# Graph attention on one core: rows 0 and 1 multiplied together strip by strip, statistics by pairs of tiles, the values' sum in four column groups, inlayer2 loaded sooner

## The chip, the core and the metric

The kernel runs on one core of one Trainium2 chip. The time is device microseconds of the whole kernel; three runs of the kernel before gave a median of 1459.9 us (1458.99 to 1459.92).

## The reference, cut to what matters

```python
N, D, H = (8192, 256, 128)
# values: h = relu(layernorm(x))            (8192 x 256)
h = jnp.maximum(_layernorm(x, axis=-1), 0.0)
# two numbers per node, from another input and small weights
g  = inlayer2 @ W.T + b
f1 = g @ w1 + b1
f2 = g @ w2 + b2
logits = f1[:, None] + f2[None, :]
bias_mat = NEG_BIG * (1.0 - (adj > 0).astype(jnp.float32))
coefs = softmax(leaky_relu(logits, 0.01) + bias_mat, axis=-1)   # 8192 x 8192
out = x + coefs @ h
```

The adjacency is 8192 x 8192 of int32 (268 MB). A node without a neighbour takes the mean of all values.

## The kernel before, in words

The exponential of a leaky ReLU of a sum splits into products of a row factor and a column factor, so the weight of a pair is `min(max(b_word, c_word), mask)` (times a factor that is put into the values). Output rows are worked on in 64 tiles of 128 ("row I"). A row has two chunks (c = 0, 1) of 4096 columns, a chunk four parts (g = 0 to 3) of 1024 columns of words and four strips. A strip (k = 0 to 7) is eight tiles of 128 neighbours.

For each row the steps are these.

- SP loads the adjacency of a chunk in four transfers of 512 KB (`load_adj`, L286) once ACT has read the chunk of the row before (`m_ready`).
- ACT turns a part of the adjacency into a mask (`mask_part`, L451). At the end of a row it scales the accumulator (`scale_rows`, L458).
- DVE makes the weights of a part (`weights`, L706) and transposes a strip of them into one of four buffers (`turn`, L716), which waits for PE to be done with the strip four earlier (`mm_done`).
- PE multiplies a strip (`products`, L892 and L894): 24 matmuls of 257 columns, three for each tile, since a weight is a bf16 high half and an f16 low half and a value is two f16 parts.
- POOL adds x and the mean's share (`finish`, L399 to L404), and SP stores the tile.

Four buffers between DVE and PE are all that decouples them. The accumulator `acc` has two halves, one for even and one for odd rows.

Ahead of the loop, and mixed with row 0, the kernel makes everything that the rows need:

- `inlayer2` comes in eight strips (L281, queues of SP and ACT, 8 transfers of 256 KB for two strips). DVE transposes each (`turn_in2`, L601), PE multiplies it (`f_of_strip`, L856: 8 matmuls, for strip k of them in two passes), ACT copies the result in two chunks (`f_to_sbuf`, L434). `chunk_f` (L632 to L637) brings f into columns and finds its maximum, which goes over PE (L877, L879) to the shifted `f2_rel` (L671). From there ACT makes the exponentials (L513, L439, L520), and DVE packs them into words (`pack`, L695 and L696).
- x comes in eight strips too. For strips 0 and 1 ACT makes sums and squares (L485). For the others DVE runs one `bn_stats` for each tile of 256 columns (`raw_stats`, L644), and `mean_var` aggregates eight tiles (L651, L653). POOL makes the inverse roots and the affine factors (`rstds`, `affine`).
- The values are made by half strips, n = 0 to 15: ACT applies the affine step and the ReLU (`values(n)`, L472, four instructions), then the f16 high part is cast (`high_of_values`: odd n on ACT, L478, even n on DVE, L683), and the low part is the difference (`low_of_values`: odd n on DVE, L690, even n on POOL, L392). POOL writes one more column of each tile (`D_column`, L385).
- In row 0 PE waits for both parts of strip k, and behind each strip's products it adds the strip's values over all nodes (`sum_of_values`, L903: 16 matmuls with 2 columns of weights and 256 columns of values). From them comes the mean (`h_sum`, L827, then L920).

The order of all this is written out by hand in each engine's program, as a list of calls (`high_of_values(0)`, `weights(0, 0, 0)`, `raw_stats(44, 48)`, ...). Engines run their lists in that order, so a wait holds up everything behind it on its engine. PE does all of row 0 and then row 1:

```python
for k in range(NS):
    if k == NS - 1:
        pe.wait_ge(scaled, I)
    if is_row(I, 0):
        for part in (hi_ready, hi_act_ready, lo_ready, lo_dve_ready, D_column_ready):
            pe.wait_ge(part, k + 1)
    products(I, par, k)
    if is_row(I, 0):
        mm = sum_of_values(k)
```

Of the kernel before, what the change touches and what calls it, by code (L numbers as in the profile page):

```python
# [35 lines left out]
P = 128  # L36
# [9 lines left out]
def graph_attention(nc, x, adj, inlayer2, W, b, w1, b1, w2, b2, out):  # L46
# [26 lines left out]
    with ExitStack() as ctx:  # L73
# [33 lines left out]
        stats = sb("stats", [P, ROWS, 6], F32)  # L107
        mv = sb("mv", [P, ROWS, 2], F32)
# [18 lines left out]
        h_sum = sb("h_sum", [2, D], F32)  # L127
# [13 lines left out]
        hs_ps = small[0:2, 1, 0:D]  # L141
# [56 lines left out]
        zeroed = sem("zeroed")  # L198
        ident_ready = sem("ident_ready")
# [24 lines left out]
        packed = sem("packed")  # L224
# [3 lines left out]
        neg_mul_ready = sem("neg_mul_ready")  # L228
        D_parts_ready = sem("D_parts_ready")
# [45 lines left out]

        block = ctx.enter_context(nc.Block())
# [33 lines left out]
        def _(sp):  # L310
# [3 lines left out]
            first_loads(sp, (0, 1))  # L314
            first_adj(sp, 0, (0, 1))
# [5 lines left out]
            def body(I, par, half):  # L321
                for n in range(NS):
                    if n % Q == Q - 1 and not is_row(I, ROWS - 1):
                        sp.wait_ge(m_ready, 8 * I + (n + 1))
# [14 lines left out]
        def _(pool):  # L339
# [6 lines left out]
            rstd_order = (0, 2, 3, 1, 4, 5, 6, 7)  # L346

            def rstds(k):
                at = slice(TS * k, TS * (k + 1))
                if k < AS:  # L350
                    pool.wait_ge(x_passes, TS * (AS + k + 1))
# [14 lines left out]
            def affine(k):  # L366
# [8 lines left out]
                else:  # L375
# [3 lines left out]
                    nc.gpsimd.tensor_tensor(h_add[:, at], mv[:, at, 0], neg_mul[:, at],  # L379
                                            ALU.mult).then_inc(h_affine_ready, 1)  # L380

# [6 lines left out]
            def low_of_values(n):  # L388

                pool.wait_ge(h_ready, HALF * (n + 1))  # L390
                pool.wait_ge(hi_ready, n // 2 + 1)
# [15 lines left out]
            for k in (0, 2, 3, 1):  # L407
                rstds(k)
            scale_D()
            for k in range(4):  # L410
                affine(k)
            low_of_values(0)
            rstds(4)
            affine(4)
            D_column(0)
            for k in range(1, NS):
                low_of_values(2 * k)
                if k + 4 < NS:
                    rstds(k + 4)
                    affine(k + 4)  # L420
                D_column(k)
# [4 lines left out]
        def _(act):  # L426
# [9 lines left out]
            def b_of_chunk(c):  # L436

                act.wait_ge(b_ps_ready, c + 1)
# [3 lines left out]
            def mask_part(I, g, c):  # L442
                if not is_row(I, 0):
                    act.wait_ge(p_ready, 8 * I + (Q * c + g - 7))
# [115 lines left out]
            for g in range(Q):  # L560
                mask_part(1, g, 1)
# [382 lines left out]
```

## Time and profile before

| | us |
|---|---|
| median of 3 runs | 1459.9 |
| the profiled execution's own time | 1460.0 |
| its span in the trace | 1458.2 |
| PE busy | 1414.1 (97%) |
| DVE busy | 1286.4 (88%) |
| ACT busy | 613.0 (42%) |
| POOL busy | 252.8 (17%) |

Between the span and the execution's own time lie 1.8 us that belong to no instruction. A row of the trace gives the start in us from the span's beginning, the length, the engine and line, the operation, what it writes and reads, how many are merged (x), and in brackets how long the engine was idle ahead of it and who ended that. Instructions of an engine overlap a little, so one of many costs the distance between two starts and not its length. PEclk is the clock that was granted to TensorE: 1.00 is 2.4 GHz and 0.50 is 1.2 GHz.

### The profile page before, as it was taken

The page shows a single profiled execution, that of the slowest core. Times are in us where ns is not written, and L with a number is a line of the kernel's source. Part 1 is how long each engine was busy: PE and PEld are TensorE (multiplying, and loading weights), DVE is VectorE, ACT ScalarE, POOL GpSimd, SP SyncE. Part 2 cuts the span into 40 slices and gives each one's busy share as a digit, 9 for nine tenths or more (in the row PEclk, how much of TensorE's full clock was granted, in tenths as well). Part 3 has the DMA queues.
Part 4 walks back from the last instruction along what each step waited for, and adds up shares of the span by engine and source line. Part 5 has one row for each costly group of instructions (what it writes and reads, how often), then busy time and mean ns, then how long its engine had stood idle before and what let it go on. Part 6 is the DMA issues. An engine that isn't in the chain of part 4 may idle for free.

```text
span 1458.2 us, 33394 instructions
## 1 busy us (share of the span) xinstructions
PE 1414.1 (97%) x12585; PEld 1248.4 (86%) x12585; DVE 1286.4 (88%) x1396; ACT 613.0 (42%) x722; POOL 252.8 (17%) x249
## 2 busy tenths in 40 slices
PE   7479999999999999999999999999999999999998
PEld 6358888888888888888888888888888888888887
DVE  5899998989898989989898989899898989898894
ACT  1794444444343444434343444444343434444430
POOL 0371111111011111111110111111011101111111
PEclk9789999999999999999999999999999999999999
DMA  9959999999999999999999999999999999999940
GB/s 293 295 117 197 229 231 232 234 231 212 210 215 207 213 209 214 210 209 215 209 211 208 215 209 212 211 214 209 210 214 209 210 207 218 209 210 212 211 106 8
DMA packets 110164, 302.36 MB, mean 207 GB/s; under 512 B 11716, under 2 KB 44612, under 8 KB 110148
## 3 DMA queue, kind: packets, MB, share of 16 engines
q1 hardware_dynamic: 100720, 291.68, 89.5%
q10 hardware_dynamic: 9428, 10.49, 2.4%
q8 instruction: 8, 0.13, 0.0%
q14 instruction: 8, 0.07, 0.0%
HBM read 293.73 MB, written 8.39 MB: 207 GB/s over the span
## 4 chain that ended last, share of the span: by engine, by line
PE 92%; ACT 2%; SPq 2%; DMA 2%; DVE 1%; issue 1%; POOL 0%; POOLq 0%; ACTq 0%; DVEq 0%
PE acc L892 61%; PE acc L894 30%; SPq L281 2%; ACT h_f L472 1%; DMA H<-in_x_dram 1%; DMA adj_sb<-in_adj_dram 1%; ACT o_room L472 1%; DVE wgt L706 0%; ACT H L478 0%; PE rp L864 0%; DVE stats L644 0%; DVE wgt L632 0%; ACT rp L451 0%; DVE H L690 0%; DVE mv L651 0%
## 5 line engine op out<-in xcount | busy, mean ns | idle before, releaser
L892 PE MATMUL acc<-H,wT 128*128 128x257 f16 x8192 | 1354.6, 273 | 19.1 <-DVE wT L716 19.1
L894 PE MATMUL acc<-H,wT 128*128 128x257 f16 x4096 | 1119.4, 273 | 0.0
L892 PEld LDWEIGHTS acc<-H,wT 128*128 128x128 bf16 x8192 | 801.6, 98 | 121.4 <-issue 21.3
L451 ACT ACTIVATE mask<-adj_sb 128x1024 bf16<-128x1024 int32 x504 | 520.0, 1054 | 552.9 <-DVE wgt L706 441.3
L716 DVE STREAM_TRANSPOSE wT<-wgt 128x1024 f32<-128x1024 f32 x512 | 633.7, 1238 | 132.9 <-PE acc L894 132.7
L706 DVE SCALAR_TENSOR_TENSOR wgt<-b_word,c_word,mask 128x1024 f32<-128x1024 f32 x504 | 627.9, 1257 | 0.0
L894 PEld LDWEIGHTS acc<-H,wT 128*128 128x128 f16 x4096 | 401.2, 98 | 50.2
L399 POOL TENSOR_TENSOR x_res<-o_room,x_res 128x256 f32<-128x256 f32 x64 | 66.4, 1037 | 1131.3 <-ACT o_room L458 1100.8
L458 ACT ACTIVATE o_room<-acc,r_den 128x256 f32<-128x256 f32 x64 | 30.3, 473 | 246.2 <-DVE r_den L735 246.2
L404 POOL TENSOR_TENSOR o_room<-o_room,x_res 128x256 f32<-128x256 f32 x64 | 81.0, 1265 | 5.3
L401 POOL TENSOR_SCALAR o_room<-h_mean,no_nb 128x256 f32<-128x256 f32 x64 | 62.1, 970 | 0.0
L856 PE MATMUL rp<-wT,h_f 128*128 128x256 f32 x128 | 30.8, 407 | 3.6 <-DVE h_f L609 3.6
L856 PEld LDWEIGHTS rp<-wT,h_f 128*128 128x128 f32 x128 | 26.3, 207 | 7.9 <-DVE h_f L609 3.7
L472 ACT ACTIVATE h_f<-H,h_add,h_mul 128x256 f32<-128x256 f32 x48 | 24.7, 587 | 0.0
L392 POOL TENSOR_TENSOR H<-h_f,H 128x1024 f16<-128x1024 f32 x8 | 20.5, 2567 | 11.1 <-DVE H L683 9.4
L644 DVE BATCH_NORM_STATS2 stats<-H 128x6 f32<-128x256 f32 x48 | 16.9, 418 | 3.7 <-DMA H<-in_x_dram 3.7
L601 DVE STREAM_TRANSPOSE wT<-wgt 128x1024 f32<-128x1024 f32 x8 | 9.5, 1222 | 8.5 <-PE rp L856 4.4
L725 DVE TENSOR_SCALAR no_nb<-acc 128x1 f32<-128x1 f32 x64 | 7.6, 118 | 9.2 <-PE acc L894 9.2
L903 PE MATMUL small<-H,D_inv_parts 128*2 128x256 f16 x128 | 15.4, 273 | 0.0
L485 ACT ACT_TABLE_LOAD x1 | 1.3, 1283 | 31.3 <-issue 31.3
L357 POOL TENSOR_TENSOR rstd<-var_eps,minus_half 128x8 f32<-128x8 f32 x8 | 13.2, 1646 | 7.0 <-DVE var_eps L653 6.8
L903 PEld LDWEIGHTS small<-H,D_inv_parts 128*2 128x2 f16 x128 | 10.1, 84 | 4.8 <-issue 1.9
(88 smaller groups left out, 159.2 us busy)
## 6 DMA issues: line engine op xcount, KB each, us to landing
adj_sb<-in_adj_dram SPq DMA_DIRECT2D x508, 512.0 KB, 8.5
x_res<-in_x_dram SPq DMA_DIRECT2D x64, 128.0 KB, 4.0
out_dram<-o_room SPq DMA_DIRECT2D x64, 128.0 KB, 4.3
H<-in_x_dram ACTq DMA_DIRECT2D x16, 256.0 KB, 12.7
H<-in_x_dram SPq DMA_DIRECT2D x16, 256.0 KB, 13.6
wgt<-in_L_gnn_inlayer_dram ACTq DMA_DIRECT2D x8, 256.0 KB, 9.8
wgt<-in_L_gnn_inlayer_dram SPq DMA_DIRECT2D x8, 256.0 KB, 10.6
adj_sb<-in_L_gnn_inlayer_dram ACTq DMA_DIRECT2D x8, 256.0 KB, 12.5
```

The lines of the kernel that those rows point to most:

```text
L281: eng.dma_start(stage[B * q:B * (q + 1), :, :], source[k // SC, k % SC, q]).then_inc(signal, 16)
L399: nc.gpsimd.tensor_tensor(x_res[:, par, :], o_raw[:, par, :], x_res[:, par, :], ALU.add).then_inc(pool_step, 1)
L401: nc.gpsimd.tensor_scalar(o_sb[:, par, :], h_mean[:, :], no_nb[:, par:par + 1], None, ALU.mult).then_inc(pool_step, 1)
L404: nc.gpsimd.tensor_tensor(o_sb[:, par, :], o_sb[:, par, :], x_res[:, par, :], ALU.add).then_inc(o_ready, 1)
L451: nc.scalar.activation(place, adj_sb[:, c, g * CQ:(g + 1) * CQ], ACT.Relu, scale=M_SCALE).then_inc(m_ready, 1)
L458: nc.scalar.activation(o_raw[:, par, :], acc[:, par, 0:D], ACT.Copy, scale=r_den[:, par:par + 1]).then_inc(scaled, 1)
L472: nc.scalar.activation(h_slot(n)[:, t, :], x_stage(n // 2)[:, j % TS, :], ACT.Relu, scale=h_mul[:, j:j + 1], bias=h_add[:, j:j + 1]).then_ ...
L706: nc.vector.scalar_tensor_tensor(out=wgt[:, c, g, :], in0=b_word[:, c * CQ:(c + 1) * CQ], scalar=c_word[:, bass.ds(Q * I + g, 1)], in1=sho ...
L716: nc.vector.transpose(wT[:, k % 4, :, :].rearrange("p t (g r) -> p g t r", g=Q), wgt[:, c, :, s * SQ:(s + 1) * SQ]).then_inc(t_ready, 1)
L856: mm = pe.matmul(rp[:, k // SC, SQ * (k % SC):SQ * (k % SC + 1)], V[:, m, :], in2T[:, k % 2, m, :], start=(m == 0), stop=(m == FM - 1))
L892: pe.matmul(acc[:, par, 0:DV], w_hi[:, k % 4, t, :], H[:, j, part, 0:DV], start=(j == 0 and part == 0), stop=False)
L894: mm = pe.matmul(acc[:, par, 0:DV], w_lo[:, k % 4, t, :], H[:, j, 0, 0:DV], start=False, stop=(j == ROWS - 1))
```

## The change

- **Order of rows 0 and 1.** Two tables set the order in which parts of weights and strips of products of rows 0 and 1 are made. PE no longer finishes row 0 first. Weights of row I go to `wgt[:, I]` for these two rows, and masks, weights, turns and values stand in new lists on ACT, DVE and POOL. All four masks of a chunk are requested by the new numbering (`nth_part`).
- **Statistics.** One `bn_stats` reads two tiles at a time, column by column alternately from one and the other, so that its statistics of even and odd elements are those of the two tiles. The aggregates (`bn_aggr`) are gone: `variance` makes `var_eps` by one instruction per strip. Numbers: 24 `bn_stats` of 512 elements for 48 of 256, and no `bn_aggr` for 48.
- **Sum of the values.** The 16 matmuls of a strip write to four column groups (PSUM partitions 0, 32, 64, 96 and the one behind each), consecutive ones to different groups. DVE zeroes the 128 partitions first, `h_sum` has 128 partitions, and the mean's matmul sums over all of them.
- **Loads.** The eight strips of inlayer2 are requested before x's strips 1 to 3. ACT requests 18 of its 256 KB transfers before its first computation, where it requested 24, and the others one or two at a time between later work. Its half of the second chunk of row 0's adjacency comes after ten steps of masks and values.
- **Who does what.** Of the 16 high parts ACT makes 12 and DVE 4 (before 8 and 8). The two parts of D and D_inv go from DVE to POOL. Chunk 1 of b is made before chunk 0.
- **Rows 0 to 2 at the seam.** The finish of row 0 stands on DVE right behind the last turn of row 1, `scale_rows(0)` on ACT behind the masks (2, g, 0), and the masks (2, g, 1) behind that.

```diff
+        two_rows = ((0, 0, 0), (0, 1, 0), (0, 2, 0), (0, 3, 0), (0, 0, 1), (0, 1, 1), (1, 0, 0), (1, 1, 0),
+                    (1, 2, 0), (1, 3, 0), (0, 2, 1), (0, 3, 1), (1, 0, 1), (1, 1, 1), (1, 2, 1), (1, 3, 1))
+        strip_order = ((0, 0), (0, 1), (0, 2), (0, 3), (1, 0), (1, 1), (1, 2), (0, 4),
+                       (1, 3), (0, 5), (1, 4), (1, 5), (0, 6), (0, 7), (1, 6), (1, 7))
...
         def first_loads(eng, quadrants):
             load_in2(eng, 0, 4, quadrants)
             load_x(eng, 0, 1, quadrants)
-            load_in2(eng, 4, 6, quadrants)
-            load_x(eng, 1, 2, quadrants)
-            load_in2(eng, 6, 8, quadrants)
-            load_x(eng, 2, 4, quadrants)
+            load_in2(eng, 4, 8, quadrants)
...
-                for j in range(first, end):
+                for j in range(first, end, 2):
                     if j == first or j % TS == 0:
                         dve.wait_ge(xs_loaded[j // TS], 64)
-                    nc.vector.bn_stats(out=stats[:, j, :], in_=x_stage(j // TS)[:, j % TS, :]).then_inc(stats_ready, 1)
-
-            def mean_var(k):
+                    nc.vector.bn_stats(out=pair_stats[:, j // 2, :],
+                                       in_=x_stage(j // TS)[:, j % TS:j % TS + 2, :].rearrange("p t d -> p d t")
+                                       ).then_inc(stats_ready, 1)
+
+            def variance(k):
...
             def products(I, par, k):
-                pe.wait_ge(t_ready, 8 * I + (k + 1))
+                pe.wait_ge(t_ready, nth_strip(I, k))
+                if is_row(I, 0):
+                    pe.wait_ge(hi_ready, k // 2 + 1)
+                    pe.wait_ge(hi_act_ready, 2 * (k + 1) - (k // 2 + 1))
+                    for part in (lo_ready, lo_dve_ready, D_column_ready):
+                        pe.wait_ge(part, k + 1)
...
-                for j in range(TS * k, TS * (k + 1)):
-                    for part in range(2):
-                        mm = pe.matmul(hs_ps, D_inv_parts[:, j, :], H[:, j, part, 0:D],
-                                       start=(j == 0 and part == 0), stop=(j == ROWS - 1 and part == 1))
+                if k == 0:
+                    pe.wait_ge(D_parts_ready, 2)
+                    pe.wait_ge(hs_zeroed, 1)
+                for part in range(2):
+                    for j in range(TS * k, TS * (k + 1)):
+                        a = B * (j % Q)
+                        mm = pe.matmul(hs_ps[a:a + 2, :], D_inv_parts[:, j, :], H[:, j, part, 0:D],
+                                       start=(j < Q and part == 0), stop=(j >= ROWS - Q and part == 1))
                 return mm
 
+            for I, k in strip_order:
+                products(I, I, k)
+                if I == 0:
+                    mm = sum_of_values(k)
+                    if k == NS - 1:
+                        mm.then_inc(h_sum_done, 1)
```

How the order moves on DVE between the last turn of inlayer2 and `f2_rel`, before:

```order
L601 STREAM_TRANSPOSE wT<-adj_sb 128x4x8x32 x8
L644 BN_STATS stats<-H 128x6 x12
L651 BN_AGGR mv<-stats 128x2 x8
L653 TENSOR_SCALAR var_eps<-mv 128x8
L632 STREAM_TRANSPOSE wgt<-mask 128x1024
L633 COPY f_col<-wgt 128x64
L635 TENSOR_REDUCE tiny<-f_col 128x1
L644 BN_STATS stats<-H 128x6 x3
L632 STREAM_TRANSPOSE wgt<-mask 128x1024
```

and in the changed kernel:

```order
L679 STREAM_TRANSPOSE wT<-adj_sb 128x4x8x32 x8
L712 STREAM_TRANSPOSE wgt<-mask 128x1024
L713 COPY f_col<-wgt 128x64
L715 TENSOR_REDUCE tiny<-f_col 128x1
L726 BN_STATS stats<-H 128x6 x4
L712 STREAM_TRANSPOSE wgt<-mask 128x1024
```

Fifteen statistics and eight aggregates stood ahead of the second transposition of `chunk_f`, and now four paired statistics do.

DVE around the first turns of the products' weights (L716), before:

```order
L690 TENSOR_TENSOR H<-h_f,H 128x4x256
L706 SCALAR_TENSOR_TENSOR wgt<-b_word,c_word,rp 128x1024
L644 BN_STATS stats<-H 128x6 x4
L716 STREAM_TRANSPOSE wT<-wgt 128x4x8x32
L706 SCALAR_TENSOR_TENSOR wgt<-b_word,c_word,rp 128x1024
L683 CAST H<-h_f 128x4x256
L690 TENSOR_TENSOR H<-o_room,H 128x4x256
```

and in the changed kernel, from its third weights (L789) to its third turn (L799):

```order
L789 SCALAR_TENSOR_TENSOR wgt<-b_word,c_word,acc 128x1024
L789 SCALAR_TENSOR_TENSOR wgt<-b_word,c_word,rp 128x1024
L769 TENSOR_TENSOR H<-h_f,H 128x4x256
L799 STREAM_TRANSPOSE wT<-wgt 128x4x8x32
L726 BN_STATS stats<-H 128x6 x2
L799 STREAM_TRANSPOSE wT<-wgt 128x4x8x32
L734 TENSOR_SCALAR var_eps<-stats 128x8
L799 STREAM_TRANSPOSE wT<-wgt 128x4x8x32
```

In both the first turn comes behind four weights and one low part. Before, weights of chunk 1, values and statistics came ahead of the second turn, and now the second and third turn follow with one paired statistics and a variance between them.

ACT's queue from the loads of inlayer2 (L281) to its first computation, before:

```order
L281 DMA wgt<-in_L_gnn_inlayer_dram 32x8x256 x8
L281 DMA H<-in_x_dram 32x8x256 x2
L281 DMA adj_sb<-in_L_gnn_inlayer_dram 32x8x256 x4
L281 DMA H<-in_x_dram 32x8x256 x2
L281 DMA adj_sb<-in_L_gnn_inlayer_dram 32x8x256 x4
L281 DMA H<-in_x_dram 32x8x256 x4
L485 ACT_TABLE_LOAD
```

and in the changed kernel:

```order
L310 DMA wgt<-in_L_gnn_inlayer_dram 32x8x256 x8
L310 DMA H<-in_x_dram 32x8x256 x2
L310 DMA adj_sb<-in_L_gnn_inlayer_dram 32x8x256 x8
L547 ACT_TABLE_LOAD
L547 ACTIVATE o_room,x_sum<-H 128x256 x8
```

The six requests for x's strips 1 to 3 no longer stand ahead of the table load.

## Rows read from the trace of the kernel before

**Rows 1.** The page: busy time, the chain, and the weight loads of the sums
```profile
PE 1414.1 (97%) x12585; PEld 1248.4 (86%) x12585; DVE 1286.4 (88%) x1396; ACT 613.0 (42%) x722; POOL 252.8 (17%) x249
...
PE 92%; ACT 2%; SPq 2%; DMA 2%; DVE 1%; issue 1%; POOL 0%; POOLq 0%; ACTq 0%; DVEq 0%
...
L903 PEld LDWEIGHTS small<-H,D_inv_parts 128*2 128x2 f16 x128 | 10.1, 84 | 4.8 <-issue 1.9
```
**Rows 2.** Windows: time; busy PE, PEld, DVE, ACT, POOL; PEclk; DMA share; GB/s
```profile
70.00:80.00 10.00, 0.36 (x2) 0.29 (x3) 9.86 (x25) 9.53 (x17) 7.26 (x9) 0.50 0.78 175
...
121.59:142.70 21.11, 21.11 (x193) 18.79 (x193) 21.11 (x23) 8.16 (x9) 2.83 (x3) 1.00 1.03 225
...
1410.80:1431.90 21.10, 21.10 (x194) 18.77 (x192) 18.89 (x20) 1.22 (x2) 3.34 (x3) 1.00 0.04 12
```
**Rows 3.** Timeline of PE, 0 to 150 us
```profile
14.29 30.84 PE L856 MATMUL rp<-wT,h_f 128*128 128x256 f32 x128 [3.62 <-DVE h_f L609]
...
79.64 0.59 PE L892 MATMUL acc<-H,wT 128*128 128x257 f16 x2 [18.23 <-DVE wT L716]
...
84.88 2.01 PE L903 MATMUL small<-H,D_inv_parts 128*2 128x256 f16 x16
...
94.97 1.91 PE L903 MATMUL small<-H,D_inv_parts 128*2 128x256 f16 x16
96.81 0.39 PE L892 MATMUL acc<-H,wT 128*128 128x257 f16 x2
...
121.59 0.40 PE L892 MATMUL acc<-H,wT 128*128 128x257 f16 x2
```
**Rows 4.** Timeline of DVE, inlayer2 to f2_rel
```profile
38.99 2.37 DVE L601 STREAM_TRANSPOSE wT<-adj_sb 128x1024 f32<-128x1024 f32 x2 [1.70 <-DMA adj_sb<-in_L_gnn_inlayer_dram]
...
50.56 0.21 DVE L633 COPY f_col<-wgt 128x64 f32<-128x64 f32 x1
...
52.02 1.23 DVE L632 STREAM_TRANSPOSE wgt<-mask 128x1024 f32<-128x1024 f32 x1
...
56.90 0.28 DVE L671 TENSOR_SCALAR f_rel<-f_col,tiny 128x64 f32<-128x64 f32 x1
```
**Rows 5.** Timeline of ACT: f's copy, four values, four masks behind a wait for adjacency
```profile
45.17 1.01 ACT L434 COPY mask<-rp 128x1024 f32<-128x1024 f32 x1
...
89.46 2.07 ACT L472 ACTIVATE h_f<-H,h_add,h_mul 128x256 f32<-128x256 f32 x4
...
135.30 3.90 ACT L451 ACTIVATE mask<-adj_sb 128x1024 bf16<-128x1024 int32 x4 [5.43 <-DMA adj_sb<-in_adj_dram]
```
**Rows 6.** Timeline of DVE: packing, first turn, and a stretch of row 0
```profile
61.89 0.72 DVE L695 TENSOR_SCALAR b_word<-wgt 128x1024 bf16<-128x1024 bf16 x1
...
64.03 0.31 DVE L695 TENSOR_SCALAR c_word<-c_f 128x256 bf16<-128x256 bf16 x1
...
78.26 1.23 DVE L716 STREAM_TRANSPOSE wT<-wgt 128x1024 f32<-128x1024 f32 x1
...
84.50 1.40 DVE L644 BATCH_NORM_STATS2 stats<-H 128x6 f32<-128x256 f32 x4
85.81 1.23 DVE L716 STREAM_TRANSPOSE wT<-wgt 128x1024 f32<-128x1024 f32 x1
86.96 0.65 DVE L683 CAST H<-h_f 128x1024 f16<-128x1024 f32 x1
87.53 1.22 DVE L690 TENSOR_TENSOR H<-h_f,H 128x1024 f16<-128x1024 f32 x1
88.67 1.40 DVE L644 BATCH_NORM_STATS2 stats<-H 128x6 f32<-128x256 f32 x4
...
112.15 3.67 DVE L706 SCALAR_TENSOR_TENSOR wgt<-b_word,c_word,mask 128x1024 f32<-128x1024 f32 x3
```
**Rows 7.** One line of DVE: a reduction that reads with a step of 32 elements
```profile
L621 DVE TENSOR_REDUCE same<-ident x1: 359/359/359, 17.0 to 17.0; 128x32 f32<-128x128 f32 x1
L624 DVE TENSOR_SCALAR mask<-mask,same x1: 288/288/288, 17.4 to 17.4; 128x128 f32<-128x128 f32 x1
```

More of the change, by code:

```diff
@@ L314, in _ @@
             first_loads(sp, (0, 1))
+            load_x(sp, 1, 4, (0, 1))
             first_adj(sp, 0, (0, 1))
@@ L405, in finish @@
                                         ALU.add).then_inc(o_ready, 1)
-            for k in (0, 2, 3, 1):
-                rstds(k)
+            rstds(0)
+            rstds(2)
+            rstds(1)
             scale_D()
-            for k in range(4):
-                affine(k)
+            affine(0)
+            affine(1)
+            parts_of_D()
             low_of_values(0)
+            D_column(0)
+            rstds(3)
+            affine(2)
             rstds(4)
+            D_column(1)
+            affine(3)
+            low_of_values(2)
             affine(4)
[L415 to L421, printed above, removed]
+            rstds(5)
+            D_column(2)
+            low_of_values(4)
+            affine(5)
+            low_of_values(6)
+            D_column(3)
+            rstds(6)
+            rstds(7)
+            D_column(4)
+            low_of_values(8)
+            affine(6)
+            D_column(5)
+            low_of_values(10)
+            affine(7)
+            D_column(6)
+            low_of_values(12)
+            D_column(7)
+            low_of_values(14)
             pool.wait_ge(h_mean_done, 1)
@@ L767, in _ @@
[L767 removed]
+            weights(0, 0, 1)
+            weights(0, 1, 1)
             raw_stats(60, 64)
[L769 to L772 removed]
+            weights(1, 0, 0)
             low_of_values(7)
[L774 to L781 removed]
@@ L782, in _ @@
-            turn(0, 5)
-            turn(0, 6)
-            low_of_values(13)
-            high_of_values(14)
-            dve.wait_ge(t_ready, 4)
-            weights(1, 0, 0)
-            turn(0, 7)
-            low_of_values(15)
+            variance(6)
             weights(1, 1, 0)
@@ L792, in _ @@
             weights(1, 3, 0)
+            turn(1, 0)
+            variance(7)
+            turn(1, 1)
+            turn(1, 2)
+            high_of_values(8)
+            weights(0, 2, 1)
+            weights(0, 3, 1)
+            low_of_values(9)
+            turn(0, 4)
+            turn(1, 3)
+            turn(0, 5)
+            weights(1, 0, 1)
+            low_of_values(11)
+            weights(1, 1, 1)
+            weights(1, 2, 1)
+            weights(1, 3, 1)
+            turn(1, 4)
+            high_of_values(12)
+            turn(1, 5)
+            turn(0, 6)
+            low_of_values(13)
+            turn(0, 7)
+            turn(1, 6)
+            low_of_values(15)
+            weights(2, 0, 0)
+            weights(2, 1, 0)
+            weights(2, 2, 0)
+            weights(2, 3, 0)
+            turn(1, 7)
+            finish_0(0, 0, 0)
+            finish_1(0, 0, 0)
+            finish_2(0, 0, 0)
+            dve.wait_ge(h_sum_done, 1)
+            nc.vector.tensor_scalar(h_sum[:, :], hs_ps, 1.0 / (H_SCALE * N), None, ALU.mult).then_inc(h_sum_ready, 1)
             def body(I, par, half):
-                if is_row(I, 0):
+                if first_two(I):
                     return
```

281 lines of the change are left out of this document (153 added, 128 removed).

## The prediction

> **What bounds the kernel now.** I read the page first. PE is busy 97% of the span and makes up 92% of the chain that ended last [rows 1]. Then I cut the span into rows. Row 1 takes 21.11 us, in which PE is busy throughout at a granted clock of 1.00, and a row near the end takes 21.10 [rows 2]. So 62 of the 64 rows run at PE's pace, and nothing in the change touches their matmuls. What the change can win lies ahead of the products of row 2, which begin at 121.59 + 21.11 = 142.7 us. Whatever moves that point moves the end by as much.
>
> The timeline of PE shows what fills the 142.7 us [rows 3]. The f of inlayer2 runs from 14.29 to 45.13. Then PE waits, for the last 18.23 us on end until 79.64. The first strip of row 0 is slow: 84.88 - 79.64 = 5.24 us for 24 matmuls, against 21.11 / 8 = 2.64 later, since the clock is at its lower level after the long idleness. Each of the eight sums of values costs 96.81 - 94.97 = 1.84 us, or 0.115 per matmul. Row 0 takes 42 us in all. From 70 to 80 us DVE is busy for 9.86 and ACT for 9.53 of 10 us, with PE's clock at 0.50 [rows 2], so the wait until 79.64 is the work of those two, and not a transfer.
>
> **Prices.** From starts that follow each other on DVE [rows 6]: one statistics (85.81 - 84.50) / 4 = 0.33, a turn 1.15, a high part 0.57, a low part 1.14, packing a chunk of b 64.03 - 61.89 = 2.14, and of c, a quarter as wide, an estimated 0.8. Weights cost 1.2 (3.67 for three). On ACT four values cost 2.0 and a mask 0.96 [rows 5], both of them the length less a tenth for overlap or divided by four.
>
> Statistics of a pair read 512 elements, which no row shows. Weights of 1024 elements take 1.2 and statistics of 256 take 0.33, so 256 more elements cost (1.2 - 0.33) / 3 = 0.29, and a pair 0.33 + 0.29 = 0.62. That is the lower bound, since the pair also reads with a step of 256 elements. What steps cost is shown by two rows. The copy of f's columns reads every sixteenth element, and its 64 elements take 0.21 us in all [rows 4], which leaves no room for a stall at each. The reduction that steps over 32 elements takes 0.359 for 128 elements, where a plain operation on as many takes 0.288 [rows 7]. Taken wholly as the price of the step, that is 0.07 / 128 an element, and 0.28 for a pair: 0.9. I take 0.62, by the copy.
>
> The Trainium skill (SBUF — State Buffer, section "SBUF: two separate sides") states that SBUF has lines of 16 bytes and that each access that goes to another line pays a penalty. By it, every one of the 512 reads would pay. No run here shows the size of such a penalty, and the copy above speaks against it.
>
> **Inlayer2 sooner: 0.** The last strip of inlayer2 arrives late, and DVE idles 1.70 us for it [rows 4]. But its turn ends at 38.99 + 2.37 = 41.36, and PE ends all eight strips at 45.13 with 3.45 us each, so it starts the last at 41.7. PE had no wait. The chain of f stays as long as it was.
>
> **To f2_rel: 6.6 sooner.** ACT copies the second half of f at 45.17 to 46.18 [rows 5], and DVE comes to it only at 52.02, since statistics and aggregates stand ahead [rows 4]. Now 4 pairs (2.5 us) stand there, behind a turn of chunk 0 at 41.4, and DVE is free before 46.2. From there: 1.8 us as before (52.02 to 53.8) for the maximum, about 1.3 for PE and the reduction of it, two pairs in the shade of PE, and `f2_rel` at 50.3 in place of 56.90.
>
> **To the first product: 8.4 sooner.** DVE's work from `f2_rel` to the first turn: small steps 0.8, 10 pairs 6.2, packing 2 x 2.14 + 0.8 = 5.1, a high part 0.6, four weights 4.8, variances 0.3. DVE comes to `low_of_values(1)` at 50.3 + 17.8 = 68.1. It waits there for ACT's high part 1. ACT's list to that point: two exponentials 0.4, b twice 2.0 and 1.0 of waiting for PE, values 0, c 0.3, four masks 3.8, values 1, 2 and 3 (with 0, 8.0), four requests 1.8, the high part 0.95, in all 18.3 after 50.4: 68.7. The low part ends at 69.9, the turn at 71.1, and PE starts at 71.2, against 79.64 (turn at 78.26, [rows 3, 6]). POOL takes the four parts of D from DVE, and with 17% busy [rows 1] it has room for them.
>
> **To the last wait of PE: DVE's list again.** PE's fifth strip is (1, 0). From 69.9 to the end of its turn DVE has five turns 5.8, eight pairs 5.0, a high part 0.6, three low parts 3.4, six weights 7.2 and variances 0.3, in all 22.3 and some 0.5 of small waits: 92.7. PE has four strips and four sums in that time, 5.24 + 3 x 2.64 + 4 sums = 17 us, and 21.5 us to do them. So PE idles some 4 us, in two or three gaps of up to 2.5, and the slow clock of the first strip costs nothing any more.
>
> **From 92.7 on PE is the bound.** It has 12 strips (31.7 us), four sums, the mean's matmul and its wait (0.7 together) and one wait that I expect at (1, 4). The second chunk of row 1's adjacency is asked for when mask (0, 3, 1) is done, at some 91, and takes 2.1 MB at 225 GB/s [rows 2], 9.3 us, and 2 to start, so that its four masks and weights come about 1.0 us late.
>
> **The sum in four column groups.** No row has it. Below, four at a time: 1.84 / 4 = 0.46 a strip. Above, no overlap even of the weight load, which takes 84 ns here [rows 1] and would stand in line with the 110 of a matmul: 3.1 a strip. I take 1.0, nearer the lower end, since the loads of today's sums are hidden already (0.115 per matmul with a load of 0.084 each). Four sums cost 4.0 us. Four more lie in PE's idle time.
>
> The Trainium skill has rules for both sides. TensorEngine Tiling (Array Packing), "Key Properties", says that a change of the tiling mode drains TensorE. TensorE: Matmul & The Clock Gate, Part 3, gives the span of tiles side by side as one matmul and 4 ns for each further tile, which would be about 0.5 us a strip. The same part states that weight loads overlap running matmuls only where the row groups differ, and here all four groups use all rows.
>
> Sum: 92.7 + 31.7 + 4.0 + 0.7 + 1.0 = 130.1, against 142.7. That is 12.6 us less. I set 0.6 aside for the small waits that such sums leave out, so 12.0. The profiled execution took 1460.0 us (the median is 1459.9, so it stands for the others). The forecast is **1448.0 us**.
>
> Row 2 onward keeps its pace. One place there is tight: PE's last strip of row 2 waits for `scale_rows(1)`, which stands behind the masks (3, g, 1). Their adjacency is asked for after the masks (2, g, 1), which now stand behind `scale_rows(0)`. From there 3.9 for masks, 11.3 for the transfer, 3.9 and 0.5: 19.6 us, and PE has two strips of row 1 less a moment, 1 us of matmul and 18.5 of row 2, about 21. A wait of the kind exists today and is hidden (5.43 us of ACT, [rows 5]).
>
> **The rivals.**
>
> *The column groups give nothing.* Each matmul of the sum waits for its own load and runs alone. The rule on row groups above says this. At 0.115 each, four sums past 92.7 cost 7.4 in place of 4.0, and the wait at (1, 4) is absorbed: 2.4 us more, 1450.4. Chance 0.14. At 3.1 a strip, PE would be busy from 71.2 on: 5.24 + 15 x 2.64 + 8 x 3.1 + 0.7 = 70.3, so 141.5 and, with small waits, no change at 1459. Chance 0.03.
>
> *The clock falls in PE's new gaps.* Gaps of 2.5 us stand between strips 2, 3 and (1, 0). If the clock goes to 1.2 GHz there, a strip costs 2.6 more: 1450.6. For it: the 18.23 us gap did this. Against: the gaps are short, and gaps of 0.2 to 0.4 in row 0 left the clock at 1.00. Chance 0.07. Later transfers of x (ACT asks for strips 1 to 3 later) would cost 1 to 4 us: chance 0.04, and better than forecast by over 2.5 us, where waits of PE vanish, 0.05.
>
> *Slower: the pairs' reads stall.* 20 of the 24 pairs lie on DVE's list ahead of 92.7. From 0.62 + 12 / 20 = 1.22 us a pair on, which is two times the plain rate, the gain is gone. At 1.6 us a pair it is 20 x 0.98 = 19.6 us, and the kernel takes 1467.6. For it: the reduction in [rows 7]. Against: the copy with a step in [rows 4]. The rule on lines of 16 bytes speaks for it too. Chance 0.05.
>
> **Numbers.** My own case, 1445.5 to 1450, has 0.62. With the cases above, faster by over 0.2% (2.9 us, about what runs of this kernel can tell from no change) has 0.92, no change 0.03 and slower 0.05. The pairs at their upper bound of 0.9 cost 20 x 0.28 = 5.6 us more, 1453.6, and two of the small cases together give about as much, so the range reaches up to 1454.5. Down it reaches to 1444.5: the sums at 0.46 and no wait at (1, 4) give 3.2 less.
>
> **What would show it.** Right: the second `chunk_f` starts at about 46, the first product at 71 to 72, PE's first strip still takes 5.2 us, PE's last gap over 0.5 us ahead of row 2 is at (1, 4), row 2 begins at 130 to 131.5, and later rows take 21.1. A pair takes 0.62 from start to start, and a strip's sum about 1.0. Wrong: a pair over 0.9, sums of 1.8, a clock under 1.00 after 80 us, rows past row 1 longer than 21.1 us, or a gain that is there at row 2 and gone at the end.

## The result, and the profile after

The changed kernel takes 1455.54 us (median of 9 runs, 1454.80 to 1455.85), the kernel before 1459.36 beside it (9 runs). The ratio is 0.997, its 95% interval 0.9962 to 0.9979. So it is faster, by 3.8 us, where I had forecast 12, and the time lies outside the range of 1444.5 to 1454.5. The profiled execution took 1455.55 us, with a span of 1453.7.

The page of the changed kernel, busy time and chain, answers to [rows 1]:

```profile
PE 1404.0 (97%) x12585; PEld 1241.2 (85%) x12585; DVE 1283.5 (88%) x1317; ACT 616.3 (42%) x726; POOL 256.6 (18%) x253
...
PE 94%; DMA 3%; ACT 2%; DVE 1%; POOL 0%; issue 0%; SPq 0%; POOLq 0%; ACTq 0%; DVEq 0%
```

DMA has 3% of the chain, 2% before. The timeline of PE from the first product on (start, length, then the idle time ahead of it and what ended that), against [rows 3]:

```profile
75.05 0.61 PE L990 MATMUL acc<-H,wT 128*128 128x257 f16 x2 [21.23 <-DVE wT L799]
...
79.34 0.61 PE L1004 MATMUL small<-H,D_inv_parts 128*2 128x256 f16 x16
81.73 0.38 PE L990 MATMUL acc<-H,wT 128*128 128x257 f16 x2 [1.79 <-DVE H L769]
...
84.47 0.61 PE L1004 MATMUL small<-H,D_inv_parts 128*2 128x256 f16 x16
85.01 0.40 PE L990 MATMUL acc<-H,wT 128*128 128x257 f16 x2
...
93.92 0.59 PE L990 MATMUL acc<-H,wT 128*128 128x257 f16 x2 [5.56 <-DVE H L769]
...
119.03 0.48 PE L990 MATMUL acc<-H,wT 128*128 128x257 f16 x2 [2.31 <-DVE wT L799]
...
137.84 0.60 PE L1015 MATMUL small<-h_sum,ones 128*128 128x256 f32 x2
138.27 0.38 PE L990 MATMUL acc<-H,wT 128*128 128x257 f16 x2
```

The first product comes 4.6 us sooner, and row 2 at 138.27 in place of 142.7. From there to the end of the span are 1315.4 us, as before (1458.2 - 142.7 = 1315.5), so the whole difference lies ahead of row 2. The 16 matmuls of a strip's sum take 85.01 - 84.47 = 0.54 up to the next product. Their weight loads show why (all 128 of them: busy us, ns of one), against [rows 1], where the same number kept the loads busy for 10.1 us:

```profile
L1004 PEld LDWEIGHTS small<-H,D_inv_parts 128*2 128x2 f16 x128 | 2.3, 81 | 1.9 <-issue 1.7
```

A load still takes 81 ns, but together they keep PEld busy for only 2.3 us, so loads for different column groups run side by side.

The last gap of PE ahead of row 2 is at strip (1, 4), and the chain of waits tells how it came about (start, length, what):

```profile
66.00 20.19 DMA adj_sb<-in_adj_dram
86.31 1.01 ACT rp L513
...
95.00 1.86 ACT rp L513 x2
96.89 0.31 SPq L315
...
98.19 11.29 DMA adj_sb<-in_adj_dram
...
115.43 0.95 ACT mask L513
116.41 1.29 DVE wgt L789
117.73 1.26 DVE wT L799
119.03 0.48 PE acc L990 x2
```

Two landings of adjacency hang on each other. ACT's masks of row 0's second chunk wait for the first, SP asks for row 1's second chunk only when the last of these masks is done (96.8), and its landing sets strip (1, 4). The chain names a transfer that starts at 66.00 for the first landing. ACT's own request starts only at 66.68, so by its start this is the last of SP's four for row 1's first chunk, which was under way at the same time. In the program the mask waits for row 0's second chunk alone (`adj_loaded[1]`), and of that the half that ACT requests was asked for last. SP's requests from row 1 on, then ACT's request for its half and both waits:

```profile
64.68 75.43 SPq L315 DMA_DIRECT2D adj_sb<-in_adj_dram  x24
```
```profile
66.68 0.80 ACTq L315 DMA_DIRECT2D adj_sb<-in_adj_dram  x2
...
85.35 1.98 ACT L513 ACTIVATE rp<-adj_sb 128x1024 f32<-128x1024 int32 x2 [5.46 <-DMA adj_sb<-in_adj_dram]
...
109.56 1.06 ACT L513 ACTIVATE mask<-adj_sb 128x1024 bf16<-128x1024 int32 x1 [2.90 <-DMA adj_sb<-in_adj_dram]
```

The same two requests in the kernel before, ACT's behind the exponentials of b and SP's for row 1:

```profile
59.90 0.80 ACTq L286 DMA_DIRECT2D adj_sb<-in_adj_dram  x2
```
```profile
72.45 68.51 SPq L286 DMA_DIRECT2D adj_sb<-in_adj_dram  x24
```

ACT's request stood 12.5 us ahead of SP's there and now stands 2.0 us behind it, so the late half also shares the transfer engines with 2.1 MB of row 1.

Two more things were not in the forecast. On DVE, three operations are long (DVE's timeline, then POOL's):

```profile
58.76 2.31 DVE L775 SCALAR_TENSOR_TENSOR c_word<-c_f,c_word 128x256 f16<-128x256 f32 x1
...
70.76 3.08 DVE L769 TENSOR_TENSOR H<-h_f,H 128x1024 f16<-128x1024 f32 x1
...
80.24 1.22 DVE L769 TENSOR_TENSOR H<-o_room,H 128x1024 f16<-128x1024 f32 x1
81.37 3.15 DVE L769 TENSOR_TENSOR H<-h_f,H 128x1024 f16<-128x1024 f32 x1
```
```profile
58.65 2.12 POOL L430 TENSOR_TENSOR H<-h_f,H 128x1024 f16<-128x1024 f32 x1 [0.77 <-DVE H L762]
...
70.64 2.12 POOL L430 TENSOR_TENSOR H<-h_f,H 128x1024 f16<-128x1024 f32 x1 [0.91 <-ACT H L540]
...
80.47 2.97 POOL L430 TENSOR_TENSOR H<-h_f,H 128x1024 f16<-128x1024 f32 x1 [1.17 <-DVE H L762]
```

And PE's granted clock falls twice more (windows of PE: time, busy, clock, DMA share, GB/s):

```profile
90.00:95.00 5.00, 1.08 (x6) 0.69 0.01 2
95.00:100.00 5.00, 5.00 (x41) 0.63 0.41 87
100.00:105.00 5.00, 5.00 (x48) 1.00 1.04 225
...
115.00:120.00 5.00, 2.69 (x33) 0.92 0.92 197
120.00:125.00 5.00, 5.00 (x35) 0.74 0.97 231
```

### The profile page after: what moved, and what is told of

It is laid out like the page before. It is cut to its first block, busy times and chain, and to the rows that moved or that the text cites. A ratio compares the mean times of both kernels' runs of the same rounds, so it can differ in the third digit from the quotient of the medians.

```text
span 1453.7 us, 33309 instructions
## 1 busy us (share of the span) xinstructions
PE 1404.0 (97%) x12585; PEld 1241.2 (85%) x12585; DVE 1283.5 (88%) x1317; ACT 616.3 (42%) x726; POOL 256.6 (18%) x253
## 4 chain that ended last, share of the span: by engine, by line
PE 94%; DMA 3%; ACT 2%; DVE 1%; POOL 0%; issue 0%; SPq 0%; POOLq 0%; ACTq 0%; DVEq 0%
PE acc L990 61%; PE acc L992 30%; DMA adj_sb<-in_adj_dram 2%; PE rp L948 2%; DMA wgt<-in_L_gnn_inlayer_dram 1%; ACT mask L513 0%; ACT o_room L547 0%; ACT rp L513 0%; ACT h_f L534 0%; ACT H L540 0%; DVE wgt L789 0%; DVE wT L679 0%; SPq L315 0%; DVE c_word L775 0%; ACT o_room L534 0%
## 5 line engine op out<-in xcount | busy, mean ns | idle before, releaser
L799 DVE STREAM_TRANSPOSE wT<-wgt 128x1024 f32<-128x1024 f32 x512 | 633.3, 1238 | 129.6 <-PE acc L992 129.5
L789 DVE SCALAR_TENSOR_TENSOR wgt<-b_word,c_word,mask 128x1024 f32<-128x1024 f32 x504 | 627.6, 1257 | 4.0 <-ACT mask L513 3.9
L726 DVE BATCH_NORM_STATS2 stats<-H 128x6 f32<-128x512 f32 x24 | 15.3, 682 | 0.1
L679 DVE STREAM_TRANSPOSE wT<-adj_sb 128x1024 f32<-128x1024 f32 x8 | 9.5, 1225 | 4.3 <-PE rp L948 4.3
L818 DVE RECIPROCAL r_den<-den 128x1 f32<-128x1 f32 x64 | 10.0, 156 | 0.1
```

Source lines behind the costliest of these rows:

```text
L679: nc.vector.transpose(in2T[:, k % 2, :, :].rearrange("p m (t s) -> p t m s", t=TS)[:, HALF * e:HALF * (e + 1), :, :], in2_stage(k)[:, HALF ...
L789: nc.vector.scalar_tensor_tensor(out=wgt[:, wgt_slot(I, c), g, :], in0=b_word[:, c * CQ:(c + 1) * CQ], scalar=c_word[:, bass.ds(Q * I + g, ...
L799: nc.vector.transpose(wT[:, wT_slot(I, k), :, :].rearrange("p t (g r) -> p g t r", g=Q), wgt[:, wgt_slot(I, c), :, s * SQ:(s + 1) * SQ]).t ...
```

## The experiments

Each is compared with the changed kernel's 1455.5 us or with the kernel it is made from. The kernel before stood beside every group and gave 1459.4 to 1459.7. "Row 2" is the start of row 2's products in the profile, from which on the changed kernel and those made from it take 1315.4 to 1315.7 us to the end of the span, and 1316.2 in one (the changed kernel with the old loads).

### The changed kernel: what holds the chain

```diff
             b_of_chunk(0)
+            first_adj(act, 1, (2, 3))
             values(0)
...
             high_of_values(2)
-            first_adj(act, 1, (2, 3))
```

> ACT's request for its half of row 0's second chunk of adjacency stands right behind the two exponentials of b again, as in the kernel before. Theory 1 (the late request is what holds the chain): in the changed kernel's trace ACT waits 5.46 us for this chunk, all its later masks stand behind that, SP asks for row 1's second chunk only when mask (0, 3, 1) is done at 96.8, and that chunk's landing at 109.5 sets PE's last wait, 2.31 us at strip (1, 4), and the clock's fall behind it (115 to 125 us at 0.92 and 0.74). With the request 13 us sooner ACT's wait goes, the landing comes about 5.4 us sooner, the wait at (1, 4) and the low clock behind it vanish; PE's strip (0, 3) starts only 0.8 sooner, since DVE's list is then what it waits for. In all 0.8 + 2.3 + 1.7 = 4.8 us: 1450.7. Theory 2 (the stretched operations of DVE hold it): DVE's list is unchanged, so at most the 0.8: 1454.7. Theory 3 (the transfers are bound by the rate of the queues, not by when they are asked for): the wait stays at 3 us or more, 1455.5.

Measured: 1450.68 us (1448.87 to 1450.82), row 2 at 133.4. ACT and PE (timelines of this run):

```profile
79.57 1.95 ACT L513 ACTIVATE rp<-adj_sb 128x1024 f32<-128x1024 int32 x2
```
```profile
92.81 0.59 PE L990 MATMUL acc<-H,wT 128*128 128x257 f16 x2 [4.71 <-DVE H L769]
```

The mask waits no more and is made 5.8 us sooner, strip (0, 3) starts only 1.1 sooner, and it is the last gap: the one at (1, 4) is gone. The gain is 4.9 by the medians. Theory 1 holds in its size and in its place. The turn of (1, 0) still ends at 97.5, 1.1 us sooner than in the changed kernel (98.6), so the late landing alone did not hold that turn up.

The second run moves three steps and changes no work:

```diff
-            high_of_values(0)
             dve.wait_ge(c_exp, 1)
             then_wait(pack(c_word[:, :], c_f32[:, :]))
+            high_of_values(0)
...
+            high_of_values(4)
             turn(0, 1)
...
+            pool.wait_ge(lo_dve_ready, 1)
             low_of_values(2)
```

> Three operations of DVE that took 2.31, 3.08 and 3.15 us, where the same form takes 0.45, 1.2 and 1.2 elsewhere, each overlapped a low part of POOL. Here c is packed ahead of the high part 0, POOL's low part 2 waits for DVE's low part 1, and DVE's high part 4 comes one turn sooner, so that POOL's low parts run beside turns, statistics and row 0's weights. Theory 1 (late request): the three operations get short and the first product comes about 3.5 us sooner, at 71.5, but the adjacency still lands when it did, so PE's wait at (1, 4) still ends at 119.0 and the time stays at 1455.5. Theory 2 (the stretched operations hold it): the time falls by 4 to 5.7 us, to 1450 to 1451.5. If the three stay long, POOL was not their cause.

Measured: 1455.26 us (1453.21 to 1456.22), row 2 at 137.8. DVE's timeline:

```profile
58.25 0.45 DVE L776 SCALAR_TENSOR_TENSOR c_word<-c_f,c_word 128x256 f16<-128x256 f32 x1
...
69.00 1.20 DVE L770 TENSOR_TENSOR H<-h_f,H 128x1024 f16<-128x1024 f32 x1
...
76.62 2.75 DVE L770 TENSOR_TENSOR H<-o_room,H 128x1024 f16<-128x1024 f32 x1
79.29 1.22 DVE L770 TENSOR_TENSOR H<-h_f,H 128x1024 f16<-128x1024 f32 x1
```

All three are short, one that now meets POOL's low part 4 (76.17, 2.12 long) has become long, and the first product comes at 71.42. So POOL was their cause. Yet nothing is won: ACT's wait for adjacency grows to 8.75 us, and the turn of (1, 0) ends at 99.2.

Both edits together:

> The early request and the three operations set apart from POOL's low parts, together. Theory 1 with both: strip (0, 3) starts at about 88 in place of 93.9, its clock stays at 1.00 or nearly, and the last wait of PE is again at (1, 4), now 3 to 4 us long, since row 1's second chunk lands at about 104. In all 5 to 7 us under the changed kernel: 1448.5 to 1450.5, so 0.5 to 2 us better than the early request alone. If the two were independent and additive it would be 4.8 + 5.7: 1445.

Measured: 1449.13 us (1448.89 to 1449.82), row 2 at 132.0. The overlaps are worth 1.5 us once the request is early, and 0.3 before. PE's last gap is again at (1, 4), 2.34 us, and the clock falls behind it (0.82 and 0.84 from 110 to 120 us). The turn of (1, 0) ends at 92.6, where the prediction had it. Together the edits are worth 6.4 us, more than the 4.9 and 0.3 of each alone, since either cause left in place still holds up that turn.

Spare matmuls in PE's gaps (forty each ahead of (0, 3) and (1, 4), then twenty ahead of (1, 4) alone):

```diff
+            def fill(k):
+                for n in range(40):
+                    pe.matmul(small[0:2, 0, 256:512], D_inv_parts[:, TS * k, :], H[:, TS * k, 0, 0:D],
+                              start=True, stop=True)
...
+                if (I, k) == (1, 4):
+                    fill(5)
                 products(I, I, k)
```

> The changed kernel with 40 spare matmuls (about 4.4 us, into PSUM that nobody reads) ahead of strip (0, 3) and 40 ahead of strip (1, 4), so that PE has no idle gap in front of either. Clock theory: strips (0, 3) and (1, 4) run at a granted clock of 1.00. The 2.6 us won at (0, 3) goes into a longer wait at (1, 4), which is set by the landing at 109.5, and the 1.7 us at (1, 4) and (1, 5) are won outright: 1453.8. If PE were the bound from 93.9 on, both would be won, 4.3 us: 1451.2. If the clock has another cause than the gaps: no gain, 1455.5, or a loss of up to 2 where the spare matmuls overrun the gap.

> The changed kernel with 20 spare matmuls (2.25 us) ahead of strip (1, 4) alone, about as long as the gap of 2.31 us there. In the run with 40 they overran it by 2.1 us, strip (1, 4) began at 121.2 in place of 119.0, and row 2 still began only 0.4 later, so that the full clock was worth 1.7. Clock theory: (1, 4) begins at 119 to 119.3 and row 2 at 136.6 to 136.9 in place of 138.3, 1.3 to 1.7 us won: 1454.0. If the gain of the clock is given back to another wait: 1455.5.

Measured: 1455.84 us (1454.72 to 1456.46) with forty and 1454.60 (1453.71 to 1454.99) with twenty. The forty ended at 121.1, 2.0 us after the turn allowed strip (1, 4), which ate the gain. What the clock costs is read from (1, 4) to row 2: 138.27 - 119.03 = 19.24 us in the changed kernel, 138.68 - 121.10 = 17.58 with forty, and 136.43 - 118.85 = 17.58 with twenty. So it costs 1.66 here. It need not fall, though: with the operations set apart, a gap of 2.37 us at the same strip left it at 1.00 from 120 to 125 us:

```profile
119.88 0.39 PE L991 MATMUL acc<-H,wT 128*128 128x257 f16 x2 [2.37 <-DVE wT L800]
```

Strip (1, 4) began 0.9 later in that run and row 2 0.5 sooner. At (0, 3) full clock won nothing, since PE then waited 1.41 us for the turn of (1, 0) instead. The profiled run with twenty was the fastest of its five (1453.71). The median shows 0.9 of the 1.66, and the scatter of the runs is 1.3.

The sum of values in one column group:

```diff
-                        a = B * (j % Q)
+                        a = 0
```

(The start and stop flags follow, for one group.)

> The changed kernel with the sum of values back in one column group, on the same two partitions for all of its matmuls. In the changed kernel's trace the 16 matmuls of a strip end 0.53 us after they start; one group took 1.84 before, so 1.3 us more a strip. Forecast by the chain: five sums lie behind strip (0, 3), of which three lie ahead of the wait of 2.31 us at (1, 4). Those three cost 3.9, of which the wait hides 2.3; the two behind it cost 2.6; the low clock behind that wait (1.7 us) goes with the wait. In all 3.9 - 2.3 + 2.6 - 1.7 = 2.5 us: 1458.0. Rival, the groups save nothing because the matmuls are hidden elsewhere: 1455.5. Rival, each of the eight sums counts in full: 10.4 us, 1466.

Measured: 1457.39 us (1456.40 to 1458.53). The groups are worth 1.9 here, close to the 2.5 of the chain and far from the 10.4 of all eight sums.

### Going on from both edits

```diff
             values(7)
-            mask_part(1, 0, 0)
             high_of_values(7)
+            mask_part(0, 2, 1)
+            mask_part(0, 3, 1)
+            mask_part(1, 0, 0)
```

Beside what is shown, mask (1, 3, 1) moves ahead of values 12 on ACT, low part 7 ahead of weights (1, 0, 0) on DVE, and the masks get a numbering of their own, by which SP waits.

> On top of the early request and the operations set apart: ACT makes row 0's masks (0, 2, 1) and (0, 3, 1) ahead of row 1's first four, where it had waited 3.3 us for row 1's first chunk, and mask (1, 3, 1) ahead of values 12; DVE makes low part 7 ahead of weights (1, 0, 0). SP's request for row 1's second chunk is then free at about 86 in place of 90.8. Theory 1 (this landing sets the last wait): the landing comes at about 98.5, ahead of ACT's need of it at 100.6, PE's waits of 0.44 and 2.34 us and the low clock behind them (1.7 us) go, strip (1, 0) comes 0.8 later. From strip (1, 0) on PE is then the bound without a gap: 93.4 + 12 x 2.64 + 4 x 0.53 + 0.43 = 127.7 for row 2 in place of 132.0, and the time 1449.1 - 4.3 = 1444.8. Rival, turn (1, 4) waits for DVE's own list: row 2 at 130 and 1447. Rival, the seam at row 2 (scale_rows, masks of row 2) gives it back: row 2 starts early, but the time stays at 1449.

Measured: 1446.68 us (1446.24 to 1447.56), row 2 at 130.3. The landing is met at 99.93 without a wait, and nothing waits behind strip (1, 0). But PE's gap of 2.60 ahead of (1, 0) lowered the clock to 0.67 from 95 to 100 us.

```diff
-            raw_stats(52, 56)
             low_of_values(3)
             low_of_values(5)
+            raw_stats(52, 56)
...
+            pool.wait_ge(lo_dve_ready, 3)
             low_of_values(4)
```

> The kernel of the row above with one collision more taken away: DVE's low parts 3 and 5 ahead of the statistics 52 to 56, and POOL's low part 4 behind both, since in the run with both changes low part 3 still took 2.76 us beside it. The operation gets 1.2 us long and the gap of PE ahead of strip (0, 1) shrinks from 2.3 to under 1 us. If the bound is ACT's list and PE behind (1, 0), as theory 1 has it, this changes the time by less than 0.5 us: 1444.8. If DVE's list still sets turn (1, 0), 1.5 us are won: 1443.3.

Measured: **1443.28 us** (1443.22 to 1443.88), ratio to before 0.9887 (0.9872 to 0.9902). PE's timeline and windows:

```profile
85.95 0.38 PE L997 MATMUL acc<-H,wT 128*128 128x257 f16 x2 [2.60 <-DVE H L776]
91.92 0.39 PE L997 MATMUL acc<-H,wT 128*128 128x257 f16 x2 [2.63 <-DVE wT L806]
```
```profile
85.00:90.00 5.00, 3.34 (x40) 1.00 0.87 194
90.00:95.00 5.00, 3.08 (x28) 1.00 1.03 226
```

The 3.4 us are more than I had given either case. Row 2 comes 3.7 sooner, at 126.62. Of this 0.5 is there at the first product already, 1.5 is the one long operation, and from (1, 0) to row 2 it is 34.70 us in place of 36.37, which is 1.7 for the clock: it stayed at 1.00 behind gaps as long as before. Why it stayed is not shown, so this half of the gain can't be put down to the edit. From strip (1, 0) on PE is the bound, as the forecast had it. This is the best kernel.

> The kernel with the early request, no overlap, row 1's request sooner and the low parts moved (1443.3), with the sum of values back in one column group. In that kernel PE has no wait behind strip (1, 0), so each of the four sums behind it counts with its full 1.31 us: 5.2, while the two in front of it lie in gaps of 2.6 us: 1448.5. In the changed kernel the same edit cost 1.9. If the groups' worth did not depend on what PE waits for: 1445.2.

Measured: 1448.80 us (1448.37 to 1449.62), 5.5 slower. The same edit cost 1.9 in the changed kernel.

> The best kernel (1443.3) with ACT's request for row 0's second chunk back behind high part 2, as in the changed kernel. Theory 1: the request goes out at about 65, the chunk lands at about 85, so mask (0, 0, 1), made at 76.8 in the best kernel, waits some 8.5 us, and all that hangs on it moves: row 1's second chunk is asked for at about 92, lands at 104, and row 2 begins 6 to 9 us later: 1449.5 to 1452. If the request's place mattered only together with the overlaps on DVE, it would cost the 4.8 it cost in the changed kernel, 1448; if the reordered masks hide it, 1443.3.

Measured: 1454.14 us (1451.79 to 1454.51), 10.9 slower, more than expected. The late chunk holds mask (0, 0, 1) for 9.13 us, PE idles 10.06 and the clock falls:

```profile
84.95 1.97 ACT L520 ACTIVATE rp<-adj_sb 128x1024 f32<-128x1024 int32 x2 [9.13 <-DMA adj_sb<-in_adj_dram]
```
```profile
92.52 0.59 PE L997 MATMUL acc<-H,wT 128*128 128x257 f16 x2 [10.06 <-DVE H L776]
```

The profiled run took 1452.12, 2.0 under the median, and in it row 2 begins 8.2 later than in the best kernel.

### The parts alone on the kernel before

The four column groups, with nothing else:

> The kernel before with nothing but the sum of values in four column groups. A strip's sum is 1.31 us shorter (1.84 to 0.53), eight of them 10.5. If PE were the only bound of row 0: 1449. But the trace of before has DVE's turns only 0.2 to 0.4 us ahead of PE in the first three strips and DVE's low part 15, behind ACT's high part, ending at 112.2; with the sums short PE waits for these. Strip (0, 7) then starts at 112.3, row 1 at 117.1 behind its own turn, 4.4 us sooner than 121.6: 1455.0. If the sums cost nothing in before, because they lay beside DVE's work: 1459.4.

The pairs alone:

> The kernel before with nothing but the statistics by pairs of tiles. DVE loses 48 x 0.35 + 3.8 for the aggregates - 24 x 0.62 = 5.7 us of work, of which 36 tiles in 48, 4.3 us, lie ahead of the first turn. If DVE's list alone sets the first product (79.64): 75.4, and 1455.2. If ACT's values and highs become the limit after some 2 us: 1457.4. If the work ahead of f2_rel is not on the path, only the 18 tiles behind it count, 2.1 us: 1457.3.

Measured: 1461.14 us (1460.49 to 1462.64) and 1461.07 (1459.15 to 1461.94), neither a gain, both about 1.6 slower by the medians, with an interval of the ratio of 1.0000 to 1.0018 that reaches down to no change. I was wrong on both. With the groups alone, the sums are short, but the scaling of `h_sum` stands on DVE behind weights and turns of row 1 and comes at 120.29, where it came at 120.54 before. DVE and PE of that run:

```profile
120.29 0.39 DVE L830 TENSOR_SCALAR h_sum<-small 128x256 f32<-128x256 f32 x1
```
```profile
120.73 1.22 PE L925 MATMUL small<-h_sum,ones 128*128 128x256 f32 x2 [5.05 <-DVE h_sum L830]
121.75 0.64 PE L895 MATMUL acc<-H,wT 128*128 128x257 f16 x2
```

Row 1 begins at 121.75, against 121.59 before [rows 3], and on a clock of 0.50 in its first 5 us. With the pairs alone the first product comes 1.7 sooner (77.90), but PE waits 1.89 at the same place, row 1 begins at 121.79, and the clock is at 0.66 there. In the new order of the work `h_sum` is needed a row later and PE does not wait for it, and there the groups count (1.9 and 5.5 us). What the pairs are worth in the new order no run shows.

The order of the loads, alone and undone:

```diff
-            load_in2(eng, 4, 6, quadrants)
-            load_x(eng, 1, 2, quadrants)
-            load_in2(eng, 6, 8, quadrants)
-            load_x(eng, 2, 4, quadrants)
+            load_in2(eng, 4, 8, quadrants)
+            load_x(eng, 1, 4, quadrants)
```

> The kernel before with nothing but the order of the loads changed, inlayer2 ahead of x's strips 1 to 3. The prediction's term is 0: PE had no wait in f, so 1459.4. A rival: x's strips 1 to 3 come later and hold ACT's sums or DVE's statistics, 1 to 3 us slower, 1460.4 to 1462.4.

Measured: 1465.24 us (1464.25 to 1465.70), 5.8 slower. ACT waits 6.07 us for adjacency where it had waited 0.47, its mask (0, 0, 1) comes 5.25 us later (78.14 for 72.89), and so does row 1 (126.84 for 121.59). This edit is not quite the order of the changed kernel: here ACT still requests all its transfers of x's strips 1 to 3 ahead of its first computation.

> The changed kernel with the loads in the order of the kernel before, on both queues. If the order of loads makes row 0's second chunk land late by itself (as on the kernel before, 5 us), the old order takes most of ACT's wait of 5.46 us away and the time falls by 3 to 4.8: 1451 to 1452.5. If the late request alone does it, the chunk still lands at 85 and the time stays at 1455.5, or 1.5 above with f's gaps.

> The best kernel with the loads of inlayer2 and of x's strips 1 to 3 in the order of the kernel before, on both queues. The prediction's term for this order was 0; on the kernel before alone it cost 5.8 us, with row 0's second chunk landing 5 us later. If the order of loads is harmful in itself, the old order gives 1 to 5 us here too: 1438 to 1442. If it only shifts which transfer is late, and the best kernel waits for none of them: 1443.3, or up to 1.5 more, since inlayer2 lands late again and f then shows gaps of 1.1 to 1.5 us as in the runs made from the kernel before.

Measured: 1455.72 us (1454.08 to 1456.58) for the changed kernel with the old order, no change, with the chunk landing as late (ACT's mask at 85.87); and 1445.36 (1443.88 to 1446.02) for the best kernel, 2.1 slower. There f waits 1.56 us for inlayer2, and the clock is at 0.72 around strip (1, 0). So the order of the loads has no part in the changed kernel's late landing, and the place of ACT's request explains it. Why the chunk lands later with the new order on the kernel before, where ACT's request went out at 58.93, stays open.

No run takes the new order of rows 0 and 1, the pairs, or the moved high parts and parts of D out of the changed kernel, so what each of them is worth there is not shown.

## Why the prediction was wrong

**Prices: right.** Four pairs took 2.50 us, so 0.62 each, and the rival of stalled reads is out:

```profile
42.28 2.50 DVE L726 BATCH_NORM_STATS2 stats<-H 128x6 f32<-128x512 f32 x4
```

By the rule of the Trainium skill (SBUF — State Buffer, "SBUF: two separate sides") each of the 512 reads would pay a penalty; the row shows none.

**To f2_rel: right** (46.15 and 50.54, against 46 and 50.3).

**To the first product: 3.9 us too early.** Where I had 71.2, it was 75.05. The pack of c and the low part were priced at their undisturbed length, and cost 1.9 us more each beside POOL. In the seven profiles with both set apart it came at 70.1 to 71.7. [Rows 6] had low parts of 1.22 only. In the kernel before, four of POOL's eight took 2.98 to 3.04, the first at 81.40 beside a low part of DVE that began at 81.17, and the others 2.13 or 2.14. So the pair already met there, with POOL the one to wait. The section of the Trainium skill just named has the rule, and I had read past it: a DVE operation with two SBUF inputs and a GpSimd operation that reads SBUF share a port pair, whichever starts first holds it for its whole length, and the other is blocked. The traces agree in both directions: POOL's part first, DVE's takes 3.08 in place of 1.20; DVE's first, POOL's takes 2.98 in place of 2.13. PE's first strip took 79.34 - 75.05 = 4.3 us, where I had 5.2.

**To the last wait of PE: this is the step that failed, together with the one before.** I had the first chain of waits as "DVE's list again", and priced ACT's requests only by their time on ACT ("four requests 1.8"). The request for row 0's second chunk moved from 59.90 to 66.68, behind SP's for row 1's first chunk, and its landing was priced nowhere. So ACT waited 5.46 us, mask (0, 3, 1), which I expected at some 91, was done at 96.9, and row 1's second chunk landed at 109.5 in place of 102.3. That set the last wait. The turn of (1, 0), at 98.6 in place of 92.7, was held by the landing and by the long operations of DVE at once: it ended at 97.5 with only the request mended, at 99.2 with only the overlaps, and at 92.6 with both. The early request gives back 4.9 of the 7.5 us that were missing, and the overlaps 1.5 more.

**From 92.7 on PE is the bound: right only without that chain.** The wait at (1, 4) was expected at 1.0 and measured 2.31. With the request and the overlaps mended it was still 2.34, so it was priced too low by itself, and the kernel took 1449.13, 1.1 over the forecast: from (1, 0) to row 2 it was 39.4 us for 38.0. With both transfers asked for sooner and the overlaps gone, strip (1, 0) starts at 91.9 and row 2 at 126.6, 34.7 us: 3.3 less than those 38.0, of which the shorter sums give 1.8 and the missing wait 1.0.

**The sum in four column groups: mis-sized.** A strip's sum costs 0.54, near the lower end of 0.46 to 3.1; I took 1.0. So the groups do run together, and the four sums behind (1, 0) cost 1.8 us less than forecast. The Trainium skill (TensorE: Matmul & The Clock Gate, Part 3) states that weight loads overlap running matmuls only where the row groups differ. Here all groups use all rows, and 16 loads of 81 ns each would alone take 1.3 us in a line. With the 2.3 us of PEld for all 128 loads a strip's 16 take 0.3, beside matmuls that run. So for column groups the trace shows otherwise, and the measurement decides.

**Inlayer2 sooner: 0 in the changed kernel** (1455.72 with it undone), but 2.1 us in the best one, and -5.8 alone.

**The rival of the falling clock** had 0.07 and 2.6 us. It happened at two gaps, of 5.56 and 2.31 us. Only that at (1, 4) counted, for 1.66, and with a gap as long it did not happen in another run.

## What to carry to other kernels

When a step moves back in an engine's program, the transfer it asks for moves too: follow it to its landing, and to every request that waits for what the landing feeds. Where a part lies behind another wait, it can be worth nothing alone (the groups, 1.7 slower by the medians) and its whole size once the wait is gone (5.5). Two causes that each hold up the same step show their worth only when both are mended (6.4 against 4.9 and 0.3). Before operations of DVE and POOL change places, look for lengths of one form that differ, such as 2.13 and 2.98: they show which operations hold each other up.

## What the runs showed of the hardware

- An operation of DVE with two inputs in SBUF (the pack of c, a low part) that starts 0.1 us behind one of POOL takes 1.9 us longer: 0.45 to 2.31, 1.20 to 3.08. The second of row 0's weights at 86.79, whose mask lies in PSUM, kept its 1.2 beside POOL's low part at 88.43, which kept its 2.13. Small operations of POOL show the same: `h_mul` (128 x 8) takes 0.20 us at 64.62 and 1.18 at 72.72, where it ends at 73.90, right behind DVE's long low part (73.84).
- A gap's length alone does not tell whether the clock falls: behind gaps of 2.31 and 2.60 it fell (0.74 and 0.67 in the next 5 us), behind 2.60 and 2.63 in the best kernel it stayed at 1.00, and so it did behind 2.37 at the strip of the first. PE's work ahead of the gaps was not the same.
- From 55 to 65 us the transfers ran at 237 and 228 GB/s in the changed kernel, and at 283 and 300 with ACT's request early, at a DMA share above 1.0 in both.
- Sixteen matmuls of the sum, spread over four column groups, take 0.54 us, where one group took 1.84. Their 128 loads of 81 ns keep PEld busy for 2.3 us, where 128 of 84 ns took 10.1.
